# Head sums of a decayed linear attention: heads spread over all feature chunks, and gate weights quantised in quarters

## The reference, cut to what matters

```python
q, k = phi(q), phi(k)
running_kv = causal_decay_scan(k * v, decay, 0)
running_ksum = causal_decay_scan(k, decay, 0)
den = clip(sum(q * running_ksum, axis=-1, keepdims=True), 1e-06, None)   # over the 32 features of a head
out = q * running_kv / den
g = sigmoid(out @ Wgate.T + bgate)
out = g * out + (1.0 - g) * v_direct
return out @ Wout.T
```

## Time and profile before

| | us |
|---|---|
| runs, median of 3 (lowest to highest) | 2666.58 (2666.1 to 2666.93) |
| profiled execution, its own time | 2664.11 |
| its span | 2661.9 |
| mean granted TensorE clock, share of full speed | 0.989 |
| busy: TensorE, its weight loads, VectorE, ScalarE, GpSimd | 2586.0, 2167.9, 1989.4, 1357.3, 397.1 |

### The profile page before, as it was taken

How to read it: one execution, slowest core, us unless ns; L and a number is a source line. 1 busy time by engine, 2 the same in 40 slices (tenths; PEclk the granted TensorE clock), 3 DMA queues, 4 the chain that set the end, 5 groups by cost and what they waited for, 6 DMA issues and landing times.

```text
span 2661.9 us, 32881 instructions
## 1 busy us (share of the span) xinstructions
PE 2586.0 (97%) x11622; PEld 2167.9 (81%) x11622; DVE 1989.4 (75%) x2736; ACT 1357.3 (51%) x1727; POOL 397.1 (15%) x278
## 2 busy tenths in 40 slices
PE   7999999999999996999999999999999699999998
PEld 6888888888888885888888887888888588888886
DVE  7788888999999885655555458987777866666664
ACT  4455555555555555333333348888888522222222
POOL 0000000000000001000000002222222143333331
PEclk9999999999999998999999999999999899999999
DMA  4011222122221223555555549777777645555552
GB/s 182 9 64 63 79 82 83 63 79 79 87 79 71 87 110 120 182 185 186 189 189 189 190 157 323 271 253 261 260 259 257 244 155 214 213 212 213 213 215 94
DMA packets 144552, 429.84 MB, mean 161 GB/s; under 512 B 72944, under 2 KB 81392, under 8 KB 104688
## 3 DMA queue, kind: packets, MB, share of 16 engines
q1 hardware_dynamic: 142192, 412.39, 42.5%
q10 hardware_dynamic: 2304, 16.78, 1.5%
HBM read 235.67 MB, written 177.21 MB: 155 GB/s over the span
## 4 chain that ended last, share of the span: by engine, by line
PE 57%; issue 1%; DVE 1%; DMA 1%; ACT 1%; POOL 0%; SPq 0%; POOLq 0%; DVEq 0%; ACTq 0%
PE pair L1963 13%; PE pair L1965 13%; PE pair L1964 13%; PE pair L2015 6%; PE pair L2016 6%; PE pair L2017 6%; PE pair L1973 0%; DMA ff_gs<-gate_ints 0%; DMA ff_q<-x_ints 0%; DMA up_products<-ff_group 0%; DVE ff_lo L1907 0%; ACT ff_group L1500 0%; ACT ff_group L1634 0%; DVE ff_stats L1919 0%; DVE ff_group L1916 0%
## 5 line engine op out<-in xcount | busy, mean ns | idle before, releaser
L1963 PE MATMUL pair<-ff_hi,wide_h 128*128 128x512 f32 x1536 | 600.1, 391 | 16.9 <-DVE ff_lo L1681 14.1
L1965 PE MATMUL pair<-ff_hi,wide_l 128*128 128x512 f32 x1536 | 598.9, 390 | 0.0
L1964 PE MATMUL pair<-ff_lo,wide_h 128*128 128x512 f32 x1536 | 598.6, 390 | 0.0
L1500 ACT ACTIVATE ff_group<-pair,ff_scales 128x512 f32<-128x512 f32 x384 | 257.3, 686 | 305.0 <-PE pair L1965 294.2
L1963 PEld LDWEIGHTS pair<-ff_hi,wide_h 128*128 128x128 f32 x1536 | 289.1, 188 | 77.4 <-DVE ff_lo L1681 14.5
L1965 PEld LDWEIGHTS pair<-ff_hi,wide_l 128*128 128x128 f32 x1536 | 288.9, 188 | 60.4
L1964 PEld LDWEIGHTS pair<-ff_lo,wide_h 128*128 128x128 f32 x1536 | 289.1, 188 | 59.7
L2015 PE MATMUL pair<-wide_h,ff_hi 128*128 128x512 f32 x768 | 299.7, 390 | 24.6 <-DVE ff_lo L1901 23.4
L931 PE MATMUL pair<-xh,wide_h 128*128 128x512 f32 x768 | 301.6, 393 | 12.8 <-DVE xl L576 12.8
L932 PE MATMUL pair<-xl,wide_h 128*128 128x512 f32 x768 | 299.9, 390 | 0.0
L935 PE MATMUL pair<-xh,wide_l 128*128 128x512 f32 x768 | 299.8, 390 | 0.0
(11 more groups left out here) (227 smaller groups left out, 4690.1 us busy)
## 6 DMA issues: line engine op xcount, KB each, us to landing
gate_products<-ff_group SPq DMA_DIRECT2D x48, 1024.0 KB, 4.0
ff_raw<-gate_products SPq DMA_DIRECT2D x48, 1024.0 KB, 5.6
up_products<-ff_group SPq DMA_DIRECT2D x48, 1024.0 KB, 4.3
ff_raw<-up_products SPq DMA_DIRECT2D x48, 1024.0 KB, 9.2
gate_ints<-ff_gs SPq DMA_DIRECT2D x48, 512.0 KB, 2.6
ff_gs<-gate_ints SPq DMA_DIRECT2D x48, 512.0 KB, 9.8
xt_raw<-in_xT SPq DMA_DIRECT2D x64, 256.0 KB, 3.3
csq<-in_ctx_rows SPq DMA_DIRECT2D x16, 1024.0 KB, 7.1
```

The lines of the kernel that those rows point to most:

```text
L1500: act.activation(group[:, g, m * T:(m + 1) * T], out_ps[(GM * g + m) % 6][:], ACT.Copy, scale=s_x).then_inc(evacuated, 1)
L1963: pe.matmul(o, wh[:, m, k], hi[:, par, k], start=(k == 0), stop=False)
L1964: pe.matmul(o, wh[:, m, k], lo[:, par, k], start=False, stop=False)
L1965: mm = pe.matmul(o, wl[:, m, k], hi[:, par, k], start=False, stop=(k == KC - 1))
```

## The change

The features are reordered on the host so that each head has 8 of its 32 features in each of the four chunks, at the same 8 partitions in all of them. The weights, the bias and the decay are reordered in the same way.

- One `head_sum` of 128x16 and one `head_bc` of 32x128 serve all chunks.
- VectorE adds the four chunks of `qks` into the first, with three new additions of 128x512 (`sum_scanned`): two behind `front_values` of chunks 1 and 2, the third right behind `front_keys` of chunk 3.
- TensorE does 4 denominator matmuls for a block where it did 16, all in one group, and later in project 1 (in the third of its four inner turns); and 1 broadcast where it did 4. All four quotients read the one bank. `qkv(s, 0)` no longer waits for `o_ready`; `qkv(s, 1)` does.
- The gate weights are quantised in twelve quarters of one tile (128x512) where there were six halves. FIRST is 2: steps 1 to 14 have a part of this work. SP and VectorE are written out in full.

```diff
-        FIRST = NB - 2 - NHALF
+        FIRST = NB - 2 - NPIECE
...
+                def sum_scanned(b, c):
+
+                    dve.wait_ge(qks_ready, KC * b + c + 1)
+                    wait(dve, qks_summed, (KC - 1) * b + c - 1)
+                    dve.tensor_tensor(qks[:, 0], qks[:, 0], qks[:, c], ALU.add).then_inc(qks_summed, 1)
...
                     front_values(b, c)
+                    sum_scanned(b, c)
...
-                        dve.wait_ge(bc_ready, n)
+                        dve.wait_ge(bc_ready, b + 1)
                         dve.wait_ge(qkv_ready, n)
-                        dve.tensor_tensor(att[:, c], att[:, c], bc_banks[c], ALU.mult).then_inc(o_ready, 1)
+                        dve.tensor_tensor(att[:, c], att[:, c], bc_bank, ALU.mult).then_inc(o_ready, 1)
...
-                        if half is not None and 0 <= half < NHALF:
-                            half_ratios(half)
+                        if piece is not None and 0 <= piece < NPIECE:
+                            piece_ratios(piece)
                         front_phi(s, 3)
                         front_keys(s, 3, par)
+                        sum_scanned(s, 3)
...
-                step(1, 1, True, True, True, due=False)
-                with dve.Fori(1, FIRST // 2 - 1) as i:
-                    for u in range(2):
-                        step(2 * i + u, u, True, True, True)
-                for b in range(FIRST - 2, NB - 1):
-                    step(b, b % 2, True, True, True, half=b - FIRST if b >= FIRST - 1 else None)
+                step(1, 1, True, True, True, due=False, piece=-1)
+                for b in range(FIRST, NB - 1):
+                    step(b, b % 2, True, True, True, piece=b - FIRST)
...
+                    if c == 1:
+                        wait(pe, o_ready, KC * b)
                     product(qk_ps[c % 2][:, 0], w_tile(0, c), x_halves)
...
-                    if c == 0:
-                        wait(pe, o_ready, KC * b)
...
-                def denominators(s, j):
-                    if j == 0:
-                        pe.wait_ge(qks_ready, KC * (s + 1))
-                    for c in range(KC):
-                        mm = pe.matmul(den_bank[:, j], qks[:, c, j * P:(j + 1) * P], head_sum[:, c],
-                                       start=(c == 0), stop=(c == KC - 1))
-                    if j == TT - 1:
-                        mm.then_inc(den_ready, 1)
+                def denominators(s):
+                    pe.wait_ge(qks_summed, (KC - 1) * (s + 1))
+                    for j in range(TT):
+                        mm = pe.matmul(den_bank[:, j], qks[:, 0, j * P:(j + 1) * P], head_sum[:], start=True, stop=True)
+                    mm.then_inc(den_ready, 1)
...
-                    pe.wait_ge(v_copied, KC * (s + 1))
-                    for c in range(KC):
-                        pe.matmul(bc_banks[c], head_bc[:, c], rec_turned[:], start=True, stop=True).then_inc(bc_ready, 1)
+                    pe.wait_ge(phi_ready, KC * (s + 1))
+                    pe.matmul(bc_bank, head_bc[:], rec_turned[:], start=True, stop=True).then_inc(bc_ready, 1)
...
-                        project(s, (1,), lambda j: denominators(s, j))
+                        project(s, (1,), lambda k: denominators(s) if k == 2 else None)
```

More of the change, by code:

```diff
@@ L169, in attention_phase, with piece_of @@
         w_new = sb("w_new", [P, WG, T])
[L170 to L175, removed]
+        blk_scale = sb("blk_scale", [P, 2, NQB])
+        blk_inv = sb("blk_inv", [P, NQB])
+        def piece_of(h):
+            return slice(h % WG, h % WG + 1)
         def chunk(ap):
@@ L199, in attention_phase @@
         group_in = [sem(f"group_in{i}") for i in range(NG)]
-        half_in, half_stored = [sem(f"half_in{i}") for i in range(2)], [sem(f"half_stored{i}") for i in range(2)]
+        piece_in, piece_stored = [sem(f"piece_in{i}") for i in range(2)], [sem(f"piece_stored{i}") for i in range(2)]
         max_ready, scale_ready, inv_ready, ratio_ready, int_ready, deq_ready, w_turned, w_high, w_low, rows_in, rows_turned = (
@@ L269, in step @@
                         load_xt(s + 1, 1)
-                        if half is not None:
-                            store_half(half)
-                            if half == NHALF - 1:
+                        if piece is not None:
+                            store_piece(piece)
+                            if piece == NPIECE - 1:
                                 load_group(0)
@@ L304, in _ @@
                 load_xt(1, 3)
-                load_half(0)
-                load_half(1)
-                with sp.Fori(0, FIRST // 2) as i:
-                    for u in range(2):
-                        step(2 * i + 1 + u, 1 - u, True)
-                for h in range(NHALF):
-                    step(FIRST + 1 + h, (FIRST + 1 + h) % 2, True, half=h)
+                load_piece(0)
+                load_piece(1)
+                for b in range(1, FIRST + 1):
+                    step(b, b % 2, True)
+                for h in range(NPIECE):
+                    step(FIRST + 1 + h, (FIRST + 1 + h) % 2, True, piece=h)
                 step(NB - 1, 1, False)
@@ L710, in largest, with step @@
                     dve.wait_ge(amax_taken, s)
-                def step(s, par, front, back, nxt, due=True, half=None):
+                def step(s, par, front, back, nxt, due=True, piece=None):
                     if front:
                         front_phi(s, 0)
-                    if half is not None and half > 0:
-                        half_scaled(half - 1)
+                    if piece is not None and piece > 0:
+                        piece_scaled(piece - 1)
                     if back:
@@ L766, in step @@
                         local_sums(s + 1, 1 - par)
-                    if half is not None and 0 <= half < NHALF:
-                        half_rounded(half)
+                    if piece is not None and 0 <= piece < NPIECE:
+                        piece_rounded(piece)
                     if back:
@@ L792, in step @@
                         second_residual(s, par)
-                    if half is not None and half + 1 < NHALF:
-                        half_scales(half + 1)
+                    if piece is not None and piece + 1 < NPIECE:
+                        piece_scales(piece + 1)
                     if front:
@@ L1064, in step @@
                         unread(14)
-                        for j in range(TT):
-                            denominators(s, j)
+                        denominators(s)
                         unread(6)
@@ L2052 @@
     a = {k: np.asarray(v) for k, v in inputs.items()}
+    spread = np.arange(HID).reshape(NH, KC, HID // (NH * KC)).transpose(1, 0, 2).reshape(HID)
     arrays = {
```

68 lines of the change are left out of this document (34 added, 34 removed).

## The result

The changed kernel takes 2637.17 us (median of 4 runs, 2635.85 to 2637.57) beside 2666.34 us for the kernel before on the same chip: a ratio of 0.9888, 95% interval 0.9876 to 0.9900, 29 us less. The profiled execution took 2635.85 us with a span of 2633.7 and a mean granted clock of 0.986.

The account below looks back on a forecast made before the run. TensorE was taken to bound the kernel, VectorE close behind. Twelve full steps 19.8 us, step 14 2.65, steps 1 and 15 7.2, less 0.6 and step 0's losses, gave 28.6 us: 2666.6 becomes 2638.0 us, range 2616 to 2652.

Parts of the forecast that it names:

- behind the last broadcast: After step 15's broadcast TensorE waits for the quotients, which come no earlier: 0.6 us taken from the gain.
- The loop: Once around a full step, residual 1 through project 3, gate and variance back to residual 1: five parts, 59.8 us.
- the second: Loop part from project 3's start to the next q product: 4.67 us, less 0.6 for broadcasts, plus 0.2, together 4.27.
- the fifth part: Loop part from the variance to residual 1, VectorE's in-order work: 38.7 us, including 0.1 less for overlap.
- The wait of TensorE: In each full step TensorE newly waits 2.0 us, nearly all at project 3's start, for residual 1.
- The floor of VectorE, 58.7: VectorE's own work in a step with a quarter: 58.7 us, 0.9 above TensorE's 57.8.
- Steps 1 and 14: Step 1 runs at TensorE's 57.8 us, gaining 3.6; step 14 lacks ratios and rounding, gaining 2.65.
- The clock in step 0: Granted clock already at 0.50 there; the gap before the reciprocals grows, costing 0.5 us more.
- The fourth rival: Clock falls in the wait ahead of project 3: 2682 us, chance 0.05; milder form 2650 us, chance 0.02.
- The signs: 128 denominator and 16 broadcast records, TensorE waiting about 2 us, VectorE over 97% busy, PEclk 1.00 behind 60 us.
- TensorE stays the bound: Rival: VectorE's work overlaps better or has slack, all 15 steps take 57.8 us: 2613 us, chance 0.11.
- VectorE binds harder: Rival: additions 2.1 us, a quarter saves only 1.5, loop of 60.7 us: 2649 us, chance 0.17.

Follow-up runs that it names:

- experiment 5: Changed kernel with the quarter's rounding moved behind residual 3, ahead of the quotients: 2632.30 us, ratio 0.9865 to the kernel before.
- 7: Changed kernel with the value scan and product of chunk 3 moved behind residual 3: 2621.78 us, ratio 0.9828 to the kernel before.
- experiment 2: Changed kernel with halves in six steps in place of quarters in twelve: 2645.10 us, ratio 0.9914 to the kernel before.
- 6: Changed kernel with the quarter's ratios and rounding both moved behind residual 3: 2632.91 us, ratio 0.9875 to the kernel before.
- experiment 8: Changed kernel with more unread matmuls around the denominators and turning of step 0: 2632.70 us, ratio 0.9870 to the kernel before.
- experiment 10: Changed kernel with the quarter's rounding done three times, values unchanged: 2659.93 us, ratio 0.9974 to the kernel before.
- experiment 4: Changed kernel with each of the four denominator matmuls issued four times, in one group: 2677.93 us, ratio 1.0039 to the kernel before.

## Why the prediction was right, and where it was not

The time was 2637.2 us for a forecast of 2638.0, inside the forecast's own case (2631 to 2645). The mechanism holds in the full steps, but the closeness of the sum is in part luck: the full steps gained nearly 5 us more than forecast, and step 1 and the end of the phase together nearly 5 us less. The measured terms go by the start of the broadcast, the mark that the prediction took from the earlier trace rows. The last one, before and after:

```profile
981.15 1.19 PE L1003 MATMUL pair<-rec_turned,head_bc 32*128 32x512 f32 x4
```

```profile
950.81 0.49 PE L1003 MATMUL pair<-rec_turned,head_bc 32*128 32x512 f32 x1
...
954.26 1.09 PE L1025 MATMUL pair<-ident_r,w_new 128*128 128x128 f32 x8 [1.94 <-DVE att L675]
```

| term | predicted, us | measured, us |
|---|---|---|
| period of a full step | 59.8 | 59.40 |
| twelve full steps, gain | 19.8 | 24.6 |
| step 14, gain | 2.65 | 2.4 |
| step 15, gain | 3.6 | 3.6 |
| step 1, gain | 3.6 | 0.4 |
| step 0 (broadcast at 59.34 before, 60.00 after) | -0.5 | -0.7 |
| behind the last broadcast | -0.6 | -2.1 |
| sum | 28.6 | 28.2 (span) |

- *TensorE was the bound, and what was taken from it counted.* Right. The quarters alone did nothing, the broadcasts put back cost 0.69 us a step.
- *VectorE's costs.* The additions took 0.46, 0.46 and 0.72 us by the starts, near the assumed 0.5, 0.5 and 0.72; a quarter's parts too (scales 1.17 for 1.19, ratios 0.62 for 0.61, rounding 0.34 for 0.4).
- *The loop.* Its five parts were predicted as 0.76, 4.27, 8.07, 7.99 and 38.7 us and measured as 0.75, 4.00, 8.07, 7.99 and 38.59. The part that was mis-sized is the second. One broadcast for four saves 0.69 us, not 0.6, since the gap behind it shrinks as well (0.24 for 0.36), and the wait for the reciprocals was made up by the turning, which overlapped more. With the 0.1 from the fifth part this is the 0.4 us per step that the forecast lacked.
- *The wait of TensorE.* "About 2 us, ahead of project 3, on residual 1": 1.74.
- *The floor of VectorE, 58.7.* 0.7 too high, and not what binds: experiments 5 and 7 took time off without taking work away. In 7 VectorE's work is 58.0 of the 58.46.
- *Steps 1 and 14.* Here the forecast failed. It said that step 1 runs "at TensorE's 57.8". Experiments 2, 5 and 6 show a second loop through the phi of chunk 3, of 59.06 us without the rounding, with the ratios or not; with the clock held (experiment 8) step 1 takes just that, and step 14 takes 59.07 where the prediction's 2.65 us of gain ask for 58.8. The prediction had its row (the wait of 0.32 there) and struck the wait out instead of following it. In full steps the two loops give the same period within a few hundredths, so the omission cost nothing there.
- *The clock in step 0.* The forecast took "0.5 us more"; it is 2.0 (experiment 8, 59.06 for 61.08). The rest of step 1's miss is the second loop, 59.06 for 57.8.
- *Behind the last broadcast.* TensorE waits 1.94 us for the quotients (1.25 before), and behind this wait the clock falls, which the forecast left out:

```profile
954.00:956.00 2.00, 1.74 (x13) 1.74 (x14) 2.00 (x5) 0.88 (x2) 1.38 (x1) 0.82 0.03 8
956.00:958.00 2.00, 2.00 (x8) 1.68 (x7) 2.00 (x6) 1.20 (x2) 0.00 (x0) 0.50 0.00 0
```

In the kernel before it is at 1.00 throughout the same place. How much of the 2.1 us each of the two costs stays open: the rest of the span differs by a few us between kernels with the same work there (1682.9 us here, 1681.4 in experiment 8, 1684.3 in experiment 5).

- *The fourth rival.* The changed kernel doesn't meet it in its steps: PEclk is 1.00 in every stretch of 2 us from 66 to 954 us. But it is a near neighbour: with a wait of 2.5 us instead of 1.74 it fell in each of six steps. The low chance of this rival rested on the idle 2 us at full clock of the earlier trace rows, and that row was misread. It is a slice of a wait of 5.07 us, behind which the same trace shows the clock at its lower level:

```profile
1021.49 3.60 PE L1034 MATMUL pair<-ident_r,qks 128*128 128x128 f32 x16 [5.07 <-DVE wide_l L801]
```

```profile
1020.00:1022.00 2.00, 0.51 (x3) 0.54 (x4) 1.90 (x8) 1.94 (x5) 0.74 (x2) 0.89 0.18 69
1022.00:1024.00 2.00, 2.00 (x11) 2.00 (x10) 1.83 (x6) 1.26 (x3) 0.34 (x1) 0.50 0.17 62
```

Here, and in experiments 2 and 10, the fall shows behind the wait and not in it, so a slice of a wait at 1.00 is no sign that the wait costs nothing. That "no loss of clock" came true in the steps is luck as far as it rested on this row.

- *The signs.* The lines have the forecast 128 and 16 records, and the waits changed sides. VectorE is busy 96.0 to 97.6% of the stretches of 100 us from 200 to 900. PEclk did not stay at 1.00 behind 60 us: it is at 0.50 until 64, and falls again behind step 15. VectorE's wait for the variance, a sign against the prediction if it grew, went from 9.5 to 10.4 us in all, 0.06 a step.
- *TensorE stays the bound* (0.11) is refuted by the wait for residual 1, *VectorE binds harder* (0.17) by the period.

Not settled: how much of the 29 us the denominators alone bring, as experiment 4 changed the clock as well. By the loops it is what the broadcasts' 10.6 leave, some 18 us with the additions' cost taken off, worked out and not measured. Sixteen denominators spread over project 1 in the changed kernel were not tried. Nor is it known what decides whether a wait costs the clock; its length alone does not, as the same wait of 2.8 us did both in experiment 10.

## What to carry to other kernels

When two engines are both nearly full, as here at 97% each, the period can be neither engine's own work but a loop that passes through both (the kernel before, with VectorE at 94%, was still bound by TensorE alone). Then follow the waits once around, list every wait that binds within a few tenths of a microsecond, and move work off the loop before making it cheaper; that took 15 us here at no cost. Time in which TensorE waits isn't free for work that stands behind the wait. And a longer wait can cost the clock as well, as it did here at 2.5 us and not at 1.7, so spreading VectorE's side work evenly can be worth more than its amount says. Look for that loss in the stretches behind the wait.

## What the runs showed of the hardware

- The granted clock fell without any idle time of TensorE, behind sixteen denominator matmuls of 16 columns in one row (0.53 in 610 to 612 us of experiment 4); the same sixteen in four groups between full products left it at 1.00. In step 0 of the kernel before, where all sixteen stand in one row too, it also fell with TensorE busy (0.79 in 55 to 56 us, busy 1.00 of 1.00).
- TensorE's wait once per step: 1.7 us never lowered the clock (twelve steps), 2.5 us did in all six steps of experiment 2, 2.8 us did in ten steps of twelve in experiment 10. Behind step 15 the wait of 1.94 us (2.18 by the weight loads, by which the others are counted) was followed by a fall in the changed kernel and not in experiment 5. Filling 1.4 us of the wait with matmuls that nobody reads kept it up.
- A GpSimd addition of 128x512, beside VectorE's scan, took 2.15 us for VectorE's 0.68, and stretched the VectorE product beside it from 0.69 to 1.61 us.
